# Expert loop of an attention and mixture-of-experts kernel: transposes by a transposing transfer, the row sum by ScalarE

## The chip, the cores and the metric

The kernel runs on one core of a Trainium2 chip. The metric is the device time of one execution in microseconds (us). The engines are TensorE (PE in the profile), VectorE (DVE), ScalarE (ACT), GpSimd (POOL) and SyncE (SP), which here only starts transfers. All run their own instruction streams and meet in semaphores.

## What is computed

Cross attention of 4 x 2048 tokens of 512 features with a short context, a residual, a layer norm, and then one of eight expert matrices for each token, the one with the highest gate score:

```python
x = x + xattn(layernorm(x), ctx_512, ctx_512, Wq, bq, Wk, bk, Wv, bv, Wo, bo)
xn = layernorm(x)
chosen = argmax(xn @ gate_w.T)                    # one of 8 for each token
out = x + xn + xn @ expert_w[chosen].T
```

## The kernel before

A first block prepares weights. A second block takes the tokens in 16 chunks of 512 and does the attention; at its end each token's row is scattered to a DRAM table `rows_by_expert`, sorted by expert, each row with its features, the two factors of its layer norm (`C_RSTD`, `C_NMR`) and its token number (`C_ID`). `row_factors` makes the factors on GpSimd, once a chunk. A third block, from line 1404 on, is the expert loop, which the change rewrites. It runs over 72 tiles (`NTILE`) of 128 rows, each with one expert, unrolled by 8 (`U`, tile t uses slot u = t mod 8). Products keep about fp32 precision by splitting each operand in two fp16 halves, hi and lo, and summing three products (`HL`). For a tile t:

- SyncE (line 1427) waits until the scatter of tile t-8 has landed (`out{u}`), and `load_rows` (lines 736 to 739) reads the tile's first row from the table `tab` in SBUF and starts the load of 128 rows into `row`. The first eight loads are started at the end of the block before.
- VectorE (line 1506) normalises it: `norm` writes `xn2` (printed `xn`) from `row`.
- TensorE (line 1461) transposes the tile in four 128x128 pieces into a PSUM bank (`tbank`, printed `mt`); ScalarE (line 1492) copies that to fp16 as `x2T_hi`; VectorE's `lo` (line 1512) makes `x2T_lo` from the bank less `x2T_hi`.
- TensorE's `mm` multiplies: 4 blocks of the contraction by 3 products, 12 matmuls of 512 columns into `obank2` (printed `mo`).
- GpSimd's `add` (line 1437) makes the row sum row + xn in place.
- VectorE's result (line 1524) is the product times a scale plus that sum, into `res`.
- GpSimd (line 1448) scatters `res` to the output rows by token number.

The order on each engine is that of the code. In its turn for tile t, VectorE does the norm of t+2, the low half of t+1, the result of t; TensorE transposes t+1 and multiplies t; GpSimd sums t+1 and scatters t.

```python
def body(t, k, u):                      # VectorE, before
    if has(t + 2):
        norm(t + 2, k + (u + 2) // U + 1, (u + 2) % U)
    if has(t + 1):
        lo(t + 1, (u + 1) % U)
```

Of the kernel before, what the change touches and what calls it, by code (L numbers as in the profile page):

```python
# [22 lines left out]
ALU = mybir.AluOpType  # L23
# [3 lines left out]
P = 128  # L27
# [6 lines left out]
KT = DM // P  # L34
# [9 lines left out]
VC = DK + 1  # L44
NTOK = B * LQ
REGION = NTOK + P
ROW = DM + 3
C_RSTD, C_NMR, C_ID = DM, DM + 1, DM + 2
NTILE = NTOK // P + E
UNROLL = 8  # L50
SCALE = 1.0 / float(DK) ** 0.5
TOP = 16384.0

# [137 lines left out]
def build(nc, x, ctx, Wq, bq, Wk, bk, Wv, bv, Wo, bo, gate_w, expert_w, out):  # L191
# [89 lines left out]
    slotf = sa("slotf", [P, TPC])  # L281


    low = -(-nc.sbuf_base // 64) * 64
    place = {"q_st": 0, "pp": 32768, "pf": 49152, "cc": 57344, "cT": 65536, "nmT": 73728, "xt3": 75776,
             "experts": 83968, "end": 149504}
    assert low + place["end"] <= nc.sbuf_usable_end
# [2 lines left out]
    def at(name, shape, dt, where, more=0):  # L290
        return nc.alloc_sbuf_tensor_at(name, shape, dt, offset=low + place[where] + more)
# [14 lines left out]
    def row_factors(m, pool, do):  # L306

        par = m.slot % 2
        wait_alone(pool, "ln2_stats", m.n + 1)
        do(nc.gpsimd.tensor_tensor(pay[:, par, :, C_RSTD], ve2[:], pows[:, 0, :], ALU.pow))  # L310
        do(nc.gpsimd.tensor_tensor(mv2[:, :, 1], mv2[:, :, 0], pay[:, par, :, C_RSTD], ALU.mult))
        nc.gpsimd.tensor_scalar(pay[:, par, :, C_NMR], mv2[:, :, 1], -1.0, None, ALU.mult)\
            .then_inc(sem("pay_stats"), 1)
# [1091 lines left out]
    U = UNROLL  # L1405
    with ExitStack() as st:
        xn2 = at("xn2", [P, U, DM], F32, "q_st", 16384)
        x2T = [at(f"x2T_{s}", [P, 2, KT, P], F16, "pf", n * 2048) for n, s in enumerate(("hi", "lo"))]
        res = at("res", [P, U, DM], F32, "pp")
        tbank = [st.enter_context(nc.psum_tensor(f"mt{i}", [P, 512], F32)) for i in range(2)]  # L1410
        obank2 = [st.enter_context(nc.psum_tensor(f"mo{i}", [P, 512], F32)) for i in range(2)]
        blk = st.enter_context(nc.Block())
        assert NTILE % U == 0
# [1 line left out]
        def tiles(eng, body):  # L1415


            with eng.Fori(0, NTILE // U - 1) as k:
                for u in range(U):
                    body(k * U + u, k, u)  # L1420
            for u in range(U):
                body(NTILE - U + u, NTILE // U - 1, u)
# [3 lines left out]

        @blk.sync
        def _(sp):
            with sp.Fori(1, NTILE // U) as k:
                for u in range(U):  # L1430

                    sp.wait_ge(sem(f"out{u}"), 16 * k)
                    load_rows(sp, k * U + u, u)

        @blk.gpsimd
        def _(pool):
            def add(t, u):

                wait_alone(pool, "xn2_ready", t + 1)
                nc.gpsimd.tensor_tensor(row[:, u, 0:DM], row[:, u, 0:DM], xn2[:, u, :], ALU.add)\  # L1440
                    .then_inc(sem("sum_ready"), 1)

            def body(t, k, u):
                if has(t + 1):
                    add(t + 1, (u + 1) % U)

                wait_alone(pool, "res_ready", t + 1 + 2)
                nc.gpsimd.indirect_dma_start(  # L1448
                    out=out_rows, out_offset=bass.IndirectOffsetOnAxis(ap=row[:, u, C_ID:C_ID + 1].bitcast(I32), axis=0),
                    in_=res[:, u, :], in_offset=None, bounds_check=NTOK - 1, oob_is_err=False)\  # L1450
                    .then_inc(sem(f"out{u}"), 16)

            add(0, 0)
            tiles(pool, body)
            for u in range(U):
                wait_alone(pool, f"out{u}", 16 * (NTILE // U))

        @blk.tensor
        def _(pe):
            HL = ((0, 0), (1, 0), (0, 1))  # L1460

            def tr(t, u):
                pe.wait_ge(sem("xn2_ready"), t + 1)
                pe.wait_ge(sem("t_used"), t + 1)
                for k in range(KT):
                    ins = nc.tensor.transpose(tbank[u % 2][:, k * P:(k + 1) * P], xn2[:, u, k * P:(k + 1) * P],  # L1466
                                              ident[:])
                ins.then_inc(sem("t_filled"), 1)

            def mm(t, u):  # L1470
                e = pe.value_load(tab[0:1, 1, bass.ds(t, 1)], min_val=0, max_val=E - 1)
                pe.wait_ge(sem("t_used"), t + 1 + 2)
                pe.wait_ge(sem("res_ready"), t + 1)
                for k in range(KT):
                    for n, (ia, ib) in enumerate(HL):
                        w = e_w[:, bass.ds(e, 1), ib, k, :].rearrange("p a n -> p (a n)")
                        ins = nc.tensor.matmul(obank2[u % 2][:, :], x2T[ia][:, u % 2, k, :], w,  # L1477
                                               start=k == 0 and n == 0, stop=k == KT - 1 and n == 2)
                ins.then_inc(sem("o_filled"), 1)

            def body(t, k, u):
                if has(t + 1):
                    tr(t + 1, (u + 1) % U)
                mm(t, u)

            tr(0, 0)
            tiles(pe, body)

        @blk.scalar
        def _(act):  # L1490
            act.nop().then_inc(sem("o_filled"), 2)

            def body(t, k, u):
                act.wait_ge(sem("t_filled"), t + 1)

                act.wait_ge(sem("o_filled"), t + 1)
                nc.scalar.activation(x2T[0][:, u % 2, :, :], tbank[u % 2][:, :].rearrange("p (k n) -> p k n", k=KT),  # L1497
                                     ACT.Copy).then_inc(sem("t_hi"), 1)

            tiles(act, body)  # L1500

        @blk.vector
        def _(dve):
            dve.nop().then_inc(sem("t_used"), 2)  # L1504
            dve.nop().then_inc(sem("res_ready"), 2)  # L1505

            def norm(t, loads, u):
# [2 lines left out]
                                        row[:, u, C_NMR:C_NMR + 1], ALU.mult, ALU.add).then_inc(sem("xn2_ready"), 1)  # L1510

            def lo(t, u):
                dve.wait_ge(sem("t_hi"), t + 1)
                nc.vector.tensor_tensor(x2T[1][:, u % 2, :, :], tbank[u % 2][:, :].rearrange("p (k n) -> p k n", k=KT),  # L1514
                                        x2T[0][:, u % 2, :, :], ALU.subtract).then_inc(sem("t_used"), 1)

            def body(t, k, u):
                if has(t + 2):
                    norm(t + 2, k + (u + 2) // U + 1, (u + 2) % U)
                if has(t + 1):  # L1520
                    lo(t + 1, (u + 1) % U)
                dve.wait_ge(sem("o_filled"), t + 1 + 2)
                dve.wait_ge(sem("sum_ready"), t + 1)
                nc.vector.scalar_tensor_tensor(out=res[:, u, :], in0=obank2[u % 2][:, :], scalar=inv[:, S_E:S_E + 1],  # L1524
                                               in1=row[:, u, 0:DM], op0=ALU.mult, op1=ALU.add)\
                    .then_inc(sem("res_ready"), 1)

            norm(0, 1, 0)
            norm(1, 1, 1)
            lo(0, 0)  # L1530
            tiles(dve, body)
    attention.close()
    es.close()
# [22 lines left out]
```

## Time and profile before

| | us |
|---|---|
| median of 3 runs | 1072.28 (1070.12 to 1076.3) |
| the profiled execution | 1070.71 |
| its span in the trace | 1068.9 |
| preparation and attention chunks, up to the last block's start | about 827 |
| expert loop, first norm to last result | 836.4 to 1059.7 |

The profile shows busy times by engine, and in forty slices of the span; a trace behind it has each instruction and what it waited for. A matmul's record is longer than the step to the next one, since matmuls overlap; so a tile's cost on TensorE is read from the chain of waits (time from one to the next) and not from the mean of one. "PEclk" is the granted clock of TensorE as a share of its full speed. Instructions of SyncE are listed as SPq, and their time is what the instruction held SyncE, not how long the transfer took; "us to landing" is from the issue to the arrival.

### The profile page before, as it was taken

To read this page: it belongs to the slowest core of one execution; us is meant where nothing else is said; L and a number is where in the kernel's file an instruction comes from. 1 tells how busy PE (TensorE), PEld (TensorE's weight loads), DVE (VectorE), ACT (ScalarE), POOL (GpSimd) and SP (SyncE) were. 2 spreads that over 40 slices of the span, in tenths; PEclk is the share of its full clock that TensorE was granted. 3 is DMA by queue.
4 is the path that set the end of the run, shared out by engine and by line. 5 is a ranking of instruction groups with operands and counts; after the bars stand their busy time and mean duration, and the time that the engine had idled before them with its cause. 6 is when DMAs were issued, how large, how long until landed. Compare 5 with 4: busy or idle time off the path is not lost. (4 is left out here: it accounts for less than half of the span.)

```text
span 1068.9 us, 27389 instructions
## 1 busy us (share of the span) xinstructions
PE 948.5 (89%) x8834; PEld 578.7 (54%) x8835; DVE 817.8 (77%) x1802; ACT 553.4 (52%) x907; POOL 554.1 (52%) x559
## 2 busy tenths in 40 slices
PE   6485799998989999898999999999976699999996
PEld 3342465656656566565665656656564355555553
DVE  7733588899878999897989999888779355566553
ACT  4236775855748567584675855766564121122210
POOL 2412434644555445564455544554555377777774
PEclk9785899999989999998999999999888799999998
DMA  8866626355453544545446255443933456565551
GB/s 240 243 161 174 146 79 157 79 141 120 129 142 91 139 109 125 142 106 142 98 131 166 68 157 119 122 121 82 276 130 120 120 172 169 162 176 170 164 173 35
DMA packets 85687, 149.53 MB, mean 140 GB/s; under 512 B 22849, under 2 KB 24693, under 8 KB 85567
## 3 DMA queue, kind: packets, MB, share of 16 engines
q1 hardware_dynamic: 73359, 111.89, 42.3%
q0 software_dynamic: 11664, 36.05, 8.8%
q8 instruction: 72, 1.18, 0.5%
q14 instruction: 48, 0.39, 0.1%
q10 hardware_dynamic: 544, 0.02, 0.0%
HBM read 58.65 MB, written 40.50 MB: 93 GB/s over the span
## 5 line engine op out<-in xcount | busy, mean ns | idle before, releaser
L827 POOL TENSOR_TENSOR p_lo<-pf,p_hi 77x512 f16<-77x512 f32 x128 | 160.3, 1260 | 194.6 <-ACT p_hi L1171 193.3
L1170 ACT ACTIVATE pf<-scoresT,exp_scale 77x512 f32<-77x512 f32 x256 | 174.9, 683 | 43.9 <-PE scoresT L1005 30.1
L1477 PE MATMUL mo<-e_w,x2T_hi 128*128 x576 | 184.2, 381 | 0.8 <-DVE x2T_lo L1514 0.8
L1171 ACT ACTIVATE p_hi<-scoresT,exp_scale 77x512 f16<-77x512 f32 x256 | 174.8, 683 | 0.0
L1497 ACT ACTIVATE x2T_hi<-mt 128x512 f16<-128x512 f32 x72 | 43.1, 598 | 183.7 <-PE mt L1466 183.7
L827 DVE TENSOR_TENSOR p_lo<-pf,p_hi 77x512 f16<-77x512 f32 x128 | 120.0, 938 | 7.1 <-ACT p_hi L1171 7.1
L1005 PE MATMUL scoresT<-q_st,k_now 97*77 97x512 f32 x256 | 112.4, 472 | 14.5 <-ACT p_hi L1171 11.0
L1524 DVE SCALAR_TENSOR_TENSOR res<-mo,inv,row 128x512 f32<-128x512 f32 x72 | 54.1, 751 | 91.3 <-PE mo L1477 91.3
L1256 DVE TENSOR_REDUCE negmax<-work 128x4 f32<-128x308 f32 x256 | 115.2, 468 | 4.4 <-PE work L1053 2.7
L1151 ACT ACTIVATE xnT_hi<-work 128x512 f16<-128x512 f32 x64 | 37.3, 596 | 146.0 <-PE work L991 145.5
L1477 PE MATMUL mo<-e_w,x2T_lo 128*128 x288 | 109.9, 382 | 0.0
L982 PE MATMUL work<-xnT_hi,wq_hi 128*128 128x512 f16 x256 | 101.3, 396 | 5.5 <-DVE xnT_lo L1234 5.5
L1448 POOL DMA_INDIRECT out<-res,row x72 | 71.5, 994 | 64.9 <-DVE xn L1509 56.7
L1021 PE MATMUL pv<-v_now_hi,p_hi 96*128 96x33 f16 x1024 | 86.7, 179 | 19.4 <-DVE cc L1242 15.9
L982 PE MATMUL work<-wo_hi,cT_hi 128*128 128x512 f16 x256 | 99.0, 387 | 1.9
L982 PE MATMUL work<-xnT_hi,wq_lo 128*128 128x512 f16 x256 | 100.2, 391 | 0.0
L982 PE MATMUL work<-xnT_lo,wq_hi 128*128 128x512 f16 x256 | 99.9, 390 | 0.0
L982 PE MATMUL work<-wo_hi,cT_lo 128*128 128x512 f16 x256 | 97.9, 382 | 0.0
L982 PE MATMUL work<-wo_lo,cT_hi 128*128 128x512 f16 x256 | 97.5, 381 | 0.0
L1021 PEld LDWEIGHTS pv<-v_now_hi,p_hi 96*128 96x128 f16 x1024 | 79.5, 96 | 33.3 <-DVE cc L1242 16.7
L1440 POOL TENSOR_TENSOR row<-row,xn 128x512 f32<-128x512 f32 x72 | 86.3, 1200 | 15.2 <-DVE xn L1509 13.7
L1229 DVE SCALAR_TENSOR_TENSOR q_lo<-work,bq_s,q_hi 128x512 fp32r<-128x512 f32 x64 | 47.9, 749 | 57.8 <-ACT q_hi L1147 57.8
(228 smaller groups left out, 2330.4 us busy)
## 6 DMA issues: line engine op xcount, KB each, us to landing
q_st<-q_hi SPq DMA_DIRECT2D x256, 128.0 KB, 2.4
row<-rows_by_expert SPq DMA_DIRECT2D x72, 257.5 KB, 3.0
xt<-in_x SPq DMA_DIRECT2D x16, 1024.0 KB, 6.3
q_st<-q_lo SPq DMA_DIRECT2D x128, 128.0 KB, 2.5
pay<-in_L_ffn_expert_w SPq DMA_DIRECT2D x8, 1024.0 KB, 7.2
er<-in_L_ffn_expert_w SPq DMA_DIRECT2D x7, 1024.0 KB, 15.4
k_next<-key_stacks SPq DMA_DIRECT2D x5, 462.0 KB, 9.8
key_stacks<-k_nat_hi SPq DMA_DIRECT2D x8, 154.0 KB, 3.3
```

The costliest lines, as they stand in the source:

```text
L827: return tt.tensor_tensor(pp[1][0:LK, g % 2, j, :], pf[:, j, :], pp[0][0:LK, g % 2, j, :], ALU.subtract)
L982: ins = nc.tensor.matmul(dst, a[ia], bm[ib], start=first and n == 0, stop=final and n == 2)
L1005: nc.tensor.matmul(sbank[n % SB][0:LK, :], k_now[0:KR, n, :], q_st[0:KR, n, :], start=True, stop=True)\
L1021: ins = nc.tensor.matmul(obank[h][:, col:col + VC], pp[ip][:, g % 2, j, t * P:(t + 1) * P], v_now[iv][:, g * HG + j, :], start=n == 0, sto ...
L1170: nc.scalar.activation(pf[:, j, :], sbank[n % SB][0:LK, :], ACT.Exp, scale=exp_scale[0:LK, :])
L1171: nc.scalar.activation(pp[0][0:LK, g % 2, j, :], sbank[n % SB][0:LK, :], ACT.Exp, scale=exp_scale[0:LK, :]).then_inc(sem("exp_done"), 1)
L1229: ins = nc.vector.scalar_tensor_tensor(out=q[1][:, at, :], in0=ps[:, :], scalar=bq_s[:, at:at + 1], in1=q[0][:, at, :].bitcast(F32), op0=A ...
L1256: return nc.vector.tensor_reduce(negmax[:, t, g * HG:(g + 1) * HG], ps[:, 0:HG * LK].rearrange("p (j s) -> p j s", j=HG), X, ALU.max, nega ...
L1440: nc.gpsimd.tensor_tensor(row[:, u, 0:DM], row[:, u, 0:DM], xn2[:, u, :], ALU.add)\
L1448: nc.gpsimd.indirect_dma_start(out=out_rows, out_offset=bass.IndirectOffsetOnAxis(ap=row[:, u, C_ID:C_ID + 1].bitcast(I32), axis=0), in_=r ...
L1477: ins = nc.tensor.matmul(obank2[u % 2][:, :], x2T[ia][:, u % 2, k, :], w, start=k == 0 and n == 0, stop=k == KT - 1 and n == 2)
L1524: nc.vector.scalar_tensor_tensor(out=res[:, u, :], in0=obank2[u % 2][:, :], scalar=inv[:, S_E:S_E + 1], in1=row[:, u, 0:DM], op0=ALU.mult, ...
```

## The change

TensorE no longer transposes. ScalarE makes the high half `x2[.., 0, ..]` in fp16 straight from `row` in SBUF (the activation applies the norm's two factors), and the row sum from the same row with the factor rstd + 1, which a fourth extra column (`C_RSTD1`) now carries; it writes the sum to `res`. GpSimd computes that column once a chunk in `row_factors`. VectorE still makes `xn2` and subtracts: the low half `x2[.., 1, ..]`, in SBUF. SyncE then starts one transposing transfer of both halves, 128 partitions x 1024 fp16 (256 KB), from `x2` to `x2T`. Both have four slots (`TB` = 4). In SyncE's turn for tile t stands the transpose of t+3, then the wait for the scatter of t-2 (`LAG` = 2), then the row load of t+6. VectorE's turn is the norm of t+4, the low half of t+3, the result of t, which now adds in place in `res`. ScalarE may write slot t mod 4 once the matmuls of t-4 are done. The rows of the table are 516 instead of 515 numbers long. The first eight tiles are written out ahead of the loop, so that a loop of seven rounds stands between two written-out rounds.

```diff
@@ -44,10 +44,12 @@
-ROW = DM + 3
-C_RSTD, C_NMR, C_ID = DM, DM + 1, DM + 2
+ROW = DM + 4
+C_RSTD, C_NMR, C_ID, C_RSTD1 = DM, DM + 1, DM + 2, DM + 3
...
+TB = 4
+LAG = 2
@@ -281,7 +283,7 @@
-    low = -(-nc.sbuf_base // 64) * 64
+    low = -(-nc.sbuf_base // 32) * 32
@@ -308,6 +310,7 @@
         do(nc.gpsimd.tensor_tensor(pay[:, par, :, C_RSTD], ve2[:], pows[:, 0, :], ALU.pow))
+        nc.gpsimd.tensor_scalar(pay[:, par, :, C_RSTD1], pay[:, par, :, C_RSTD], 1.0, None, ALU.add)
@@ -1405,9 +1408,9 @@
     U = UNROLL
     with ExitStack() as st:
         xn2 = at("xn2", [P, U, DM], F32, "q_st", 16384)
-        x2T = [at(f"x2T_{s}", [P, 2, KT, P], F16, "pf", n * 2048) for n, s in enumerate(("hi", "lo"))]
+        x2 = at("x2", [P, TB, 2, DM], F16, "pf")
+        x2T = at("x2T", [P, TB, 2 * KT, P], F16, "xt3")
         res = at("res", [P, U, DM], F32, "pp")
-        tbank = [st.enter_context(nc.psum_tensor(f"mt{i}", [P, 512], F32)) for i in range(2)]
         obank2 = [st.enter_context(nc.psum_tensor(f"mo{i}", [P, 512], F32)) for i in range(2)]
         blk = st.enter_context(nc.Block())
         assert NTILE % U == 0
@@ -1415,7 +1418,9 @@
         def tiles(eng, body):
 
 
-            with eng.Fori(0, NTILE // U - 1) as k:
+            for u in range(U):
+                body(u, 0, u)
+            with eng.Fori(1, NTILE // U - 1) as k:
                 for u in range(U):
                     body(k * U + u, k, u)
             for u in range(U):
@@ -1426,23 +1431,28 @@
 
         @blk.sync
         def _(sp):
-            with sp.Fori(1, NTILE // U) as k:
-                for u in range(U):
-
-                    sp.wait_ge(sem(f"out{u}"), 16 * k)
-                    load_rows(sp, k * U + u, u)
+            def transpose(t, k, u):
+
+                wait_alone(sp, "x2_lo", t + 1)
+                sp.dma_start(x2T[:, u % TB, :, :], x2[:, u % TB, :, :].rearrange("p h n -> p (h n)"), transpose=True)\
+                    .then_inc(sem(f"x2T_in{u % TB}"), 16)
+
+            def body(t, k, u):
+                if has(t + TB - 1):
+                    transpose(t + TB - 1, k, (u + TB - 1) % U)
+                if isinstance(t, int) and not 0 <= t - LAG < NTILE - U:
+                    return
+                v = (u - LAG) % U
+                wait_alone(sp, f"out{v}", 16 * (k + (u - LAG) // U + 1))
+                load_rows(sp, t - LAG + U, v)
+
+            for t in range(TB - 1):
+                transpose(t, 0, t)
+            tiles(sp, body)
 
         @blk.gpsimd
         def _(pool):
-            def add(t, u):
-
-                wait_alone(pool, "xn2_ready", t + 1)
-                nc.gpsimd.tensor_tensor(row[:, u, 0:DM], row[:, u, 0:DM], xn2[:, u, :], ALU.add)\
-                    .then_inc(sem("sum_ready"), 1)
-
             def body(t, k, u):
-                if has(t + 1):
-                    add(t + 1, (u + 1) % U)
 
                 wait_alone(pool, "res_ready", t + 1 + 2)
                 nc.gpsimd.indirect_dma_start(
@@ -1450,7 +1460,6 @@
                     in_=res[:, u, :], in_offset=None, bounds_check=NTOK - 1, oob_is_err=False)\
                     .then_inc(sem(f"out{u}"), 16)
 
-            add(0, 0)
             tiles(pool, body)
             for u in range(U):
                 wait_alone(pool, f"out{u}", 16 * (NTILE // U))
@@ -1459,49 +1468,38 @@
         def _(pe):
             HL = ((0, 0), (1, 0), (0, 1))
 
-            def tr(t, u):
-                pe.wait_ge(sem("xn2_ready"), t + 1)
-                pe.wait_ge(sem("t_used"), t + 1)
-                for k in range(KT):
-                    ins = nc.tensor.transpose(tbank[u % 2][:, k * P:(k + 1) * P], xn2[:, u, k * P:(k + 1) * P],
-                                              ident[:])
-                ins.then_inc(sem("t_filled"), 1)
-
-            def mm(t, u):
+            def body(t, k8, u):
                 e = pe.value_load(tab[0:1, 1, bass.ds(t, 1)], min_val=0, max_val=E - 1)
-                pe.wait_ge(sem("t_used"), t + 1 + 2)
+                pe.wait_ge(sem(f"x2T_in{u % TB}"), 16 * (k8 * (U // TB) + u // TB + 1))
                 pe.wait_ge(sem("res_ready"), t + 1)
                 for k in range(KT):
                     for n, (ia, ib) in enumerate(HL):
                         w = e_w[:, bass.ds(e, 1), ib, k, :].rearrange("p a n -> p (a n)")
-                        ins = nc.tensor.matmul(obank2[u % 2][:, :], x2T[ia][:, u % 2, k, :], w,
+                        ins = nc.tensor.matmul(obank2[u % 2][:, :], x2T[:, u % TB, ia * KT + k, :], w,
                                                start=k == 0 and n == 0, stop=k == KT - 1 and n == 2)
                 ins.then_inc(sem("o_filled"), 1)
 
-            def body(t, k, u):
-                if has(t + 1):
-                    tr(t + 1, (u + 1) % U)
-                mm(t, u)
-
-            tr(0, 0)
             tiles(pe, body)
 
         @blk.scalar
         def _(act):
-            act.nop().then_inc(sem("o_filled"), 2)
+            act.nop().then_inc(sem("o_filled"), 2 + TB)
 
             def body(t, k, u):
-                act.wait_ge(sem("t_filled"), t + 1)
-
-                act.wait_ge(sem("o_filled"), t + 1)
-                nc.scalar.activation(x2T[0][:, u % 2, :, :], tbank[u % 2][:, :].rearrange("p (k n) -> p k n", k=KT),
-                                     ACT.Copy).then_inc(sem("t_hi"), 1)
+                act.wait_ge(sem(f"row_in{u}"), 16 * (k + 1))
+
+                act.wait_ge(sem("o_filled"), t + 1 + 2)
+                nc.scalar.activation(x2[:, u % TB, 0, :], row[:, u, 0:DM], ACT.Identity,
+                                     scale=row[:, u, C_RSTD:C_RSTD + 1], bias=row[:, u, C_NMR:C_NMR + 1])\
+                    .then_inc(sem("x2_hi"), 1)
+                nc.scalar.activation(res[:, u, :], row[:, u, 0:DM], ACT.Identity,
+                                     scale=row[:, u, C_RSTD1:C_RSTD1 + 1], bias=row[:, u, C_NMR:C_NMR + 1])\
+                    .then_inc(sem("sum_ready"), 1)
 
             tiles(act, body)
 
         @blk.vector
         def _(dve):
-            dve.nop().then_inc(sem("t_used"), 2)
             dve.nop().then_inc(sem("res_ready"), 2)
 
             def norm(t, loads, u):
@@ -1510,24 +1508,26 @@
                                         row[:, u, C_NMR:C_NMR + 1], ALU.mult, ALU.add).then_inc(sem("xn2_ready"), 1)
 
             def lo(t, u):
-                dve.wait_ge(sem("t_hi"), t + 1)
-                nc.vector.tensor_tensor(x2T[1][:, u % 2, :, :], tbank[u % 2][:, :].rearrange("p (k n) -> p k n", k=KT),
-                                        x2T[0][:, u % 2, :, :], ALU.subtract).then_inc(sem("t_used"), 1)
+                dve.wait_ge(sem("x2_hi"), t + 1)
+                dve.wait_ge(sem("xn2_ready"), t + 1)
+                nc.vector.tensor_tensor(x2[:, u % TB, 1, :], xn2[:, u, :], x2[:, u % TB, 0, :], ALU.subtract)\
+                    .then_inc(sem("x2_lo"), 1)
 
             def body(t, k, u):
-                if has(t + 2):
-                    norm(t + 2, k + (u + 2) // U + 1, (u + 2) % U)
-                if has(t + 1):
-                    lo(t + 1, (u + 1) % U)
-                dve.wait_ge(sem("o_filled"), t + 1 + 2)
+                if has(t + TB):
+                    norm(t + TB, k + (u + TB) // U + 1, (u + TB) % U)
+                if has(t + TB - 1):
+                    lo(t + TB - 1, (u + TB - 1) % U)
+                dve.wait_ge(sem("o_filled"), t + 1 + 2 + TB)
                 dve.wait_ge(sem("sum_ready"), t + 1)
                 nc.vector.scalar_tensor_tensor(out=res[:, u, :], in0=obank2[u % 2][:, :], scalar=inv[:, S_E:S_E + 1],
-                                               in1=row[:, u, 0:DM], op0=ALU.mult, op1=ALU.add)\
+                                               in1=res[:, u, :], op0=ALU.mult, op1=ALU.add)\
                     .then_inc(sem("res_ready"), 1)
 
-            norm(0, 1, 0)
-            norm(1, 1, 1)
-            lo(0, 0)
+            for t in range(TB):
+                norm(t, 1, t)
+            for t in range(TB - 1):
+                lo(t, t)
             tiles(dve, body)
     attention.close()
     es.close()
```

On SyncE, in the loop: before, one tile's turn is

```order
L738 ISA [waits out3]
L738 TENSOR_LOAD tab
L738 ISA x2
L739 ISA
L739 DMA row<-rows_by_expert 128x515
```

and now, with `x_10803` the tile `x2`,

```order
L1437 DMA_TRANSPOSE x2T<-x_10803 128x8x128 [waits x2_lo]
L741 ISA [waits out3]
L741 TENSOR_LOAD tab
L741 ISA x2
L742 ISA
L742 DMA row<-rows_by_expert 128x516
```

The transpose, with its wait for VectorE's low half, stands ahead of the wait for the scatter and ahead of the row load.

On VectorE, in the loop: before, one turn is

```order
L1509 TENSOR_SCALAR xn_10794<-row 128x512 [waits row_in4]
L1514 TENSOR_TENSOR x2T_lo<-mt,x2T_hi 128x512 [waits t_hi]
...
L1524 SCALAR_TENSOR_TENSOR res<-mo,inv,row 128x512 [waits sum_ready,o_filled]
```

and now two turns are

```order
L1507 TENSOR_SCALAR xn_10802<-row 128x512 [waits row_in1]
L1513 TENSOR_TENSOR x_10803<-xn_10802,x_10803 128x512 [waits xn2_ready,x2_hi]
L1521 REGISTER_ALU
L1523 SCALAR_TENSOR_TENSOR res<-mo,inv,res 128x512 [waits sum_ready,o_filled]
L1507 TENSOR_SCALAR xn_10802<-row 128x512 [waits row_in2]
L1513 TENSOR_TENSOR x_10803<-xn_10802,x_10803 128x512 [waits xn2_ready,x2_hi]
L1521 REGISTER_ALU
L1523 SCALAR_TENSOR_TENSOR res<-mo,inv,res 128x512 [waits sum_ready,o_filled]
```

The order of the three kinds is the same. What they wait for differs, and the norm is now four tiles ahead of the result of its turn instead of two, the low half three instead of one.

## Rows read from the trace of the kernel before

**Rows 1.** Busy time of each engine by window; the windows of the expert loop and around.

```profile
core 0: us, PE busy (x) PEld busy (x) DVE busy (x) ACT busy (x) POOL busy (x), PEclk, DMA share, GB/s
760.00:800.00 40.00, 33.12 (x428) 25.37 (x427) 30.93 (x68) 27.23 (x47) 21.39 (x25) 0.83 0.63 226
800.00:815.00 15.00, 12.56 (x82) 7.12 (x81) 13.04 (x46) 5.33 (x8) 7.17 (x8) 1.00 0.29 109
...
840.00:845.00 5.00, 5.00 (x18) 2.18 (x17) 1.02 (x2) 0.12 (x1) 0.00 (x0) 0.65 0.00 0
...
850.00:1050.00 200.00, 200.00 (x1059) 108.56 (x1057) 119.16 (x198) 39.48 (x66) 145.09 (x134) 1.00 0.56 167
```

**Rows 2.** Chain of waits, 740 to 900 and 1050 to 1069: start, us, what.

```profile
836.34 0.09 issue
836.43 0.56 DVE xn L1509
836.98 0.04 issue
837.03 1.13 PE mt L1466 x4
838.16 0.02 issue
838.18 0.61 ACT x2T_hi L1497
838.78 0.02 issue
838.81 0.70 DVE x2T_lo L1514
839.51 0.32 issue
839.83 4.57 PE mo L1477 x12
844.41 0.44 PE mt L1466 x4
844.84 2.59 PE mo L1477 x12
847.43 0.44 PE mt L1466 x4
...
1053.68 5.19 PE mo L1477 x24
```

**Rows 3.** Groups of instructions by line, 850 to 1050: busy us, mean ns, idle before.

```profile
L1440 POOL TENSOR_TENSOR row<-row,xn 128x512 f32<-128x512 f32 x67 | 80.4, 1200 | 1.5
L1448 POOL DMA_INDIRECT out<-res,row x67 | 66.6, 994 | 54.2 <-DVE xn L1509 49.1 <-issue 5.0
...
L1524 DVE SCALAR_TENSOR_TENSOR res<-mo,inv,row 128x512 f32<-128x512 f32 x66 | 49.6, 751 | 80.6 <-PE mo L1477 80.6
L1514 DVE TENSOR_TENSOR x2T_lo<-mt,x2T_hi 128x512 f16<-128x512 f32 x66 | 45.1, 683 | 0.0
```

**Rows 4.** SyncE: line 739 and its landings, the first eight loads, scatter waits and landings.

```profile
L739 SPq DMA_DIRECT2D row<-rows_by_expert x72: 337/338/368, 827.4 to 1040.5; - x72
DMA to landing us min/median/max: 2.5/3.0/4.1
827.35 8.12 SPq L739 DMA_DIRECT2D row<-rows_by_expert  x8
SPq L738 <- DMA out<-res,row: 111.2, 48, 3.7
out<-res,row POOLq DMA_INDIRECT x67, 2.9
```

**Rows 5.** Other transfers that SyncE starts: ns min/median/max, their landings (us).

```profile
L401 SPq DMA_DIRECT2D bvec<-in_L_xattn_bv x1: 1135/1135/1135, 2.8 to 2.8; - x1
L401 SPq DMA_DIRECT2D bvec<-in_L_xattn_bo x1: 819/819/819, 4.0 to 4.0; - x1
L401 SPq DMA_DIRECT2D bvec<-in_L_xattn_bq x1: 2747/2747/2747, 4.8 to 4.8; - x1
DMA to landing us min/median/max: 5.5/7.4/8.7
L868 SPq DMA_DIRECT2D q_st<-q_hi x256: 585/597/1938, 64.3 to 752.0; - x128
q_st<-q_hi SPq DMA_DIRECT2D x256, 128.0 KB, 2.4
```

**Rows 6.** DMA queues, 850 to 1050: packets, MB, share of sixteen engines.

```profile
q1 hardware_dynamic: 9216, 16.88, 35.2%
q0 software_dynamic: 5280, 16.46, 21.2%
issues: line engine op xcount, KB each, median us to landing
row<-rows_by_expert SPq DMA_DIRECT2D x64, 257.5 KB, 2.9
```

**Rows 7.** Single lines (ns min/median/max) and one wait, whole span.

```profile
L1509 DVE TENSOR_SCALAR xn<-row x72: 536/539/566, 836.4 to 1050.9; 128x512 f32<-128x512 f32 x72
L1120 ACT ACTIVATE xn<-xt,nmr,rstd x60: 797/809/817, 70.3 to 703.3; 128x512 f32<-128x512 f32 x60
L827 DVE TENSOR_TENSOR p_lo<-pf,p_hi x128: 669/678/2653, 90.0 to 783.8; 77x512 f16<-77x512 f32 x128
L312 POOL TENSOR_SCALAR pay<-mv x16: 231/232/245, 181.2 to 817.5; 128x4 f32<-128x4 f32 x16
POOL pay L310 <- DVE ve L1362: 92.8, 14, 7.7
```

**Rows 8.** Timeline of TensorE at the loop's start: start, us, line, operation.

```profile
840.23 0.63 PE L1477 MATMUL mo<-e_w,x2T_lo 128*128 x1
840.66 1.06 PE L1477 MATMUL mo<-e_w,x2T_hi 128*128 x2
841.51 0.63 PE L1477 MATMUL mo<-e_w,x2T_lo 128*128 x1
```

## The prediction

> **What bounds the kernel now.** First the windows [rows 1]. From 850 to 1050 us, TensorE is busy 200.00 of 200 us at a granted clock of 1.00 (2.4 GHz), and VectorE 119, ScalarE 39, GpSimd 145 us: the expert loop is TensorE's alone. Then the chain of waits [rows 2]. It goes back through the loop without one gap: 4 transposes (0.44 us), 12 matmuls (2.59 us), and again, 3.03 us a tile. Where no transpose is left, two tiles take 5.19 us, 2.59 each. So the change takes off 0.44 us of TensorE a tile, at most 71 x 0.44 = 31 us, if nothing else becomes the bound. Then what runs beside it: the groups by line [rows 3] and SyncE [rows 4]. SyncE waits 111 us in 48 waits for scatters to land, so it has room, and a row tile is asked for as soon as its slot is free. A slot is freed some 4.6 us after its tile's last matmul (result, GpSimd's turn, landing), so the row for eight tiles on is asked for some four tiles before VectorE reads it, and a landing of about 3 us costs nothing. This last point is what the change alters.
>
> **TensorE's part.** 288 transposes go, with the ScalarE copy and the VectorE subtraction that read them from PSUM. The 12 matmuls stay. Floor: 2.59 us a tile, 10 of 72 tiles surely near it (the first eight have their rows already; the last have none to wait for): 10 x -0.44 = -4.4 us.
>
> **ScalarE, VectorE, GpSimd.** ScalarE makes two tiles from the row, each at most 0.81 us (the activation with scale and bias columns from SBUF [rows 7]): 1.6 us a tile, under any period below. VectorE keeps three instructions, 0.54 + 0.68 + 0.75 = 1.97 us [rows 3, 7]. The subtraction now reads SBUF; the same form with an SBUF source took 0.68 [rows 7], so I keep it. GpSimd loses 1.20 us a tile and only scatters, 0.99. None of them becomes the bound. The sum `row + xn` as one activation costs nothing that anything waits for: it is ready two to three tiles before the result needs it. GpSimd's extra small instruction in the chunks (0.23 us each, 16 times, by its twin [rows 7]) hides in GpSimd's 93 us of waiting for VectorE's statistics [rows 7]; only the last one delays the last scatter and the first row load: +0.2 us.
>
> **SyncE's part, where the forecast is decided.** Each tile SyncE now starts a transpose, then waits for a scatter, reads a table entry, and starts a row load, in that order. Two things follow.
>
> (1) *A ring.* The transpose of tile t+3 waits for VectorE's low half of t+3. Behind it on SyncE stands the row load of t+6. VectorE reads that row (norm of t+6) two turns later and, in its own order, just ahead of the low half of t+5, and the transpose of t+5 waits for that. So two tiles cannot take less than: SyncE's time in the transpose instruction (call it h) + the way to the row load's issue + its landing + norm + low half + hand-overs. The way to the issue is 0.76: eight row loads span 8.12 us from the first issue to the last's end, (8.12 - 0.34) / 7 = 1.11 each, less the issue's 0.34 [rows 4]. Landing is 3.0 in the median, 2.5 to 4.1 [rows 4]. Norm 0.54, low half 0.68 [rows 7, 3]. Three hand-overs at about 0.05, as between the chain's first links [rows 2]: 0.15. Without h that is 5.13 us. The ring equals today's 3.03 us a tile at h = 6.06 - 5.13 = 0.93 us. The wait for the scatter of t-2 doesn't add: its result follows the low half of t+1 on VectorE, two turns (6.1 us and more) ahead of the transpose of t+3, and needs 0.75 and a landing of 2.9 [rows 3, 4], so it has landed over 2 us before SyncE asks.
>
> (2) *h itself.* No row shows a transposing transfer. Bounds: below, the plain row load of the same 256 KB, 0.34 us. Above, a transfer cut into many small pieces. The transpose must address 128 x 8 pieces of 256 bytes; the nearest rows by number of pieces are the three bias vectors, 512 pieces each, which held SyncE 0.82, 1.14 and 2.75 us [rows 5]. A copy between SBUF places of 64 pieces (32 partitions, two each) held it 0.60 [rows 5]. I take the mean of the three, 1.57, since the count of pieces and not the bytes sets these rows apart (0.34 for 257.5 KB, 1.14 for 2 KB). Then the ring is (1.57 + 5.13) / 2 = **3.35 us a tile**. SyncE's own load is 1.57 + 1.11 = 2.68, less than that.
>
> On the price of such a transfer the Trainium skill speaks twice. Its page "Advanced Engine Details and Errata", X-Bar Transpose (TRN2), has transposing transfers as fast as regular ones; by that h would be 0.34 and the fast rival below would hold. The same page of the Trainium skill, DMA Advanced Topics, calls the hardware queue's transpose efficiency "Worse"; that speaks for the forecast. No row here tells them apart.
>
> **Start and end.** Today the first matmul stands 3.40 us after the first norm (836.43 to 839.83) [rows 2]. After: four norms 2.16, one low half 0.68, then the first landing. An SBUF-to-SBUF copy lands in 2.4 with h = 0.60 [rows 5], so 3.4 with h = 1.57: 6.3 us, +2.9. Both begin at TensorE's low clock (0.65 in the mean of 840 to 845 [rows 1]; the first tile takes 4.57 us either way). The end is as before: last result, scatter, landing.
>
> **Sum**, against the profiled execution's own 1070.71 us (span 1068.9): 62 tiles x (3.35 - 3.03) = +19.8; ten tiles -4.4; start +2.9; GpSimd +0.2; together +18.5, 1089.2. That execution stood 1.6 under the median of the runs, so **1091 us**.
>
> **Rivals.**
> *Fast: the transpose is issued like a copy* (faster than before). It decides from h below 0.93. At h = 0.60 the ring is 5.73 / 2 = 2.86: 62 x -0.17 = -10.5, -4.4, start +1.9, +0.2: -12.8, 1060 on the median. At 0.34 with a landing of 2.9 it is 2.69: -21.1 - 4.4 + 2.1 = -23.4, 1049. Below that the DMA engines hold: per tile the row loads take 35.2% of 200 us over 64 = 1.10 us of all sixteen, the scatters 21.2% over 67 = 0.63 [rows 6], a transpose of as many bytes about 1.10 if it costs as a load does, together 2.83. For it: SyncE's waits show that a plain issue leaves room. Against it: the three bias rows. Chance 0.18.
> *Slow: h at the upper row.* At 2.75 the ring is 3.94 and SyncE alone 3.86, so both agree: 62 x 0.91 = +56.4, -4.4, start +4.0, +0.2: 1128. With the landing at its longest, 4.1, since three streams now share the engines, 4.49: 1162. For it: sixteen engines at 2.83 of 3.35 us are 84% used against 56% now [rows 1], so landings get longer, not shorter. Chance 0.20.
> *Clock.* TensorE now stands 0.76 of 3.35 us. If the granted clock falls for stretches, a tile takes up to 5.1 (twelve at 0.43, the step between matmuls at 1.2 GHz [rows 8]) and is the bound itself. One tile in eight so: 9 x 1.75 = +16, 1107. Rows speak both ways: at 84% busy the clock stayed 1.00 (800 to 815), at 83% it was 0.83 (760 to 800) [rows 1]. Chance 0.08.
> *One transpose at a time.* If a transpose were worked off block by block and the next waited for it, the landing is the period. The many-piece rows landed in 7.4 us in the median [rows 5]: 72 x 4.4 = +315, 1387. The Trainium skill, "VectorE: DVE Perf Modes", The three transpose paths, gives 1309 ns for one 128x128 block; eight would be 10.5 us, and by that the time would be some 1610. Nothing in this trace bears it out. Chance 0.04.
>
> **How the numbers follow.** Forecast 0.50 (h 0.9 to 2.2, 1072 to 1110), fast 0.18, slow 0.20, clock 0.08, one at a time 0.04. Over or under 0.5% (5.4 us) is about what a measurement of this kernel can tell from no change. Of the forecast's half, 0.05 lie within that and 0.02 below it, so faster 0.20, same 0.05, slower 0.75. The range leaves out the lower third of the fast case and the upper half of the slow one with the last: 1052 to 1150.
>
> **What the changed kernel's profile would show.** Right: the TensorE groups show the matmuls alone, 72 x 12, with idle time in front of them put down to the transposing transfer; SyncE's time in the transpose near 1.6 us; the row load issued within 1 us of the transpose's end; VectorE idle ahead of the norm, waiting for the row load, and no longer ahead of the result; the same pattern each two tiles, 6.7 us apart. Wrong: TensorE unbroken at 2.59 a tile (h small, or rows that come earlier than I count); or SyncE never waiting, so that its own instructions are the bound (h above 2.8); or the granted clock below 1.00 in the loop; or gaps in the attention chunks, where I count nothing. What would make the forecast wrong above all is h, which I have from transfers of another kind.

## The result and the profile after

The changed kernel takes 1104.89 us (median of 4 runs, 1097.27 to 1107.31) against 1071.20 beside it: 1.030 times the time of before, 95% interval 1.023 to 1.037. It is slower by 34 us; the forecast was 1091, 19 us slower, with a range of 1052 to 1150. Ratios leave out disturbed executions, which concerns one run in this document (the 1075.77 us among the eight of the version with every second tile).

The windows of the changed kernel (us; busy time and count of each engine, granted clock, DMA share, GB/s), to be held against [rows 1]:

```profile
core 0: us, PE busy (x) PEld busy (x) DVE busy (x) ACT busy (x) POOL busy (x), PEclk, DMA share, GB/s
...
860.00:1060.00 200.00, 160.93 (x702) 64.44 (x700) 103.40 (x172) 87.36 (x116) 58.09 (x58) 0.99 0.90 223
```

TensorE is busy 161 of 200 us instead of all 200, with its clock at 0.99 (its upper level, 2.4 GHz), and the DMA engines are busy 0.90 of the time instead of 0.56. 58 scatters in 200 us make 3.45 us a tile, where the kernel before needs 3.03. The DMA engines' share times this pace, 0.90 x 3.45 = 3.10 us, is what they spend on a tile; that product is used again below.

Its chain of waits in the middle of the loop (start, us, what), to be held against the unbroken PE rows of [rows 2]:

```profile
949.52 1.27 SPq L1437
950.78 0.05 issue
...
950.89 0.06 SPq L741
950.99 0.60 SPq L741
951.62 0.15 SPq L741
...
952.04 3.03 DMA row<-rows_by_expert
955.12 0.07 issue
955.23 0.05 issue
955.30 0.25 issue
955.55 0.70 DVE x L1513
956.28 0.05 issue
956.33 1.26 SPq L1437
```

This is the ring, link by link: SyncE starts a transpose (line 1437, 1.27 us); reads the table (line 741); starts the row load, which lands 3.03 us later; VectorE makes the norm (its record runs from 955.09 to 955.64; in the chain the short pieces and the 0.25 stand for it) and the low half; and SyncE starts the transpose two tiles on. From 949.52 to 956.33 are 6.81 us for two tiles. TensorE doesn't occur in these links. In the chain of the whole loop its matmuls make up 7%, at the start, at the end and once near 964.

Who waits for whom, same stretch (us in total, times, longest):

```profile
POOL out L1458 <- DVE res L1523: 142.4, 58, 3.7
ACT x L1492 <- DMA row<-rows_by_expert: 110.0, 56, 3.1
DVE xn L1507 <- DMA row<-rows_by_expert: 95.8, 57, 2.8
...
PE mo L1478 <- DVE res L1523: 36.0, 34, 1.8
PE mo L1478 <- DMA x2T<-x: 2.7, 2, 2.2
```

VectorE now waits 95.8 us for row loads, which cost it nothing in the loop before, and no longer for TensorE (80.6 us in [rows 3]). TensorE waits for VectorE's results, since these stand behind the norms in VectorE's order; the transposed tiles themselves are there in time (2.7 us).

SyncE waits for little, and only for VectorE's low half:

```profile
SPq L208 <- DVE x L1513: 19.4, 30, 1.2
```

So SyncE's own turn takes (200 - 19.4) / 58 = 3.11 us. The ring, at 3.45, is the bound, but SyncE and the DMA engines (3.10) stand close below it, and both above the 3.03 of the kernel before.

The added instructions (ns min/median/max), SyncE's and ScalarE's:

```profile
L1437 SPq DMA_TRANSPOSE x2T<-x x72: 1232/1268/1476, 845.0 to 1086.4; - x72
DMA to landing us min/median/max: 3.1/3.5/5.4
...
L741 SPq TENSOR_LOAD <-tab x72: 264/615/962, 832.4 to 1078.5; - x72
...
L1492 ACT ACTIVATE x<-row x72: 797/813/817, 842.4 to 1083.8; 128x512 f16<-128x512 f32 x72
```

### The profile page after: what moved, and what is told of

Its sections match the earlier page's. It is cut to its first block and busy times, and to the rows that moved or that the text cites. A ratio compares the mean times of both kernels' runs of the same rounds, so it can differ in the third digit from the quotient of the medians.

```text
span 1103.8 us, 26830 instructions
## 1 busy us (share of the span) xinstructions
PE 925.5 (84%) x8546; PEld 533.6 (48%) x8547; DVE 818.7 (74%) x1802; ACT 619.4 (56%) x979; POOL 472.5 (43%) x503
## 5 line engine op out<-in xcount | busy, mean ns | idle before, releaser
L1478 PE MATMUL mo<-e_w,x2T 128*128 x864 | 200.0, 385 | 61.1 <-DVE res L1523 40.2
L1478 PEld LDWEIGHTS mo<-e_w,x2T 128*128 128x128 f16 x864 | 80.4, 99 | 180.6 <-issue 95.8
L1492 ACT ACTIVATE x<-row 128x512 f16<-128x512 f32 x72 | 58.5, 813 | 142.9 <-DMA row<-rows_by_expert 123.6
L1507 DVE TENSOR_SCALAR xn<-row 128x512 f32<-128x512 f32 x72 | 39.4, 551 | 115.4 <-DMA row<-rows_by_expert 107.5
L1024 PE MATMUL pv<-v_now_lo,p_hi 96*128 96x33 f16 x1024 | 85.8, 178 | 0.0
```

Source lines behind the costliest of these rows:

```text
L1024: ins = nc.tensor.matmul(obank[h][:, col:col + VC], pp[ip][:, g % 2, j, t * P:(t + 1) * P], v_now[iv][:, g * HG + j, :], start=n == 0, sto ...
L1478: ins = nc.tensor.matmul(obank2[u % 2][:, :], x2T[:, u % TB, ia * KT + k, :], w, start=k == 0 and n == 0, stop=k == KT - 1 and n == 2)
L1492: nc.scalar.activation(x2[:, u % TB, 0, :], row[:, u, 0:DM], ACT.Identity, scale=row[:, u, C_RSTD:C_RSTD + 1], bias=row[:, u, C_NMR:C_NMR ...
```

## Experiments

### The row load one tile less ahead

```diff
-LAG = 2
+LAG = 3
```

> The same number the other way: the row load in SyncE's turn for t is that of t+5. Ring theory: the ring spans one tile, 6.8 us a tile instead of 3.4, 64 x 3.4 = +218, about 1320 us, the DMA engines half idle. Rival, the DMA engines or SyncE are the bound: the same transfers and instructions, about 1105 to 1120.

It took 1301.81 us in its one run, where the ring theory had about 1320 and the rival 1105 to 1120. Its chain:

```profile
942.87 1.27 SPq L1437
...
944.44 0.61 SPq L741
...
945.52 2.65 DMA row<-rows_by_expert
...
948.65 0.70 DVE x L1513
949.38 0.05 issue
949.43 1.27 SPq L1437
```

The same links, 6.56 us, now for one tile instead of two. The rival is out: the instructions and transfers are the same, the DMA engines are busy 0.47 of the time, and the time is 197 us more. Only where the row load stands in SyncE's order has changed. TensorE's granted clock is 0.76 in the mean there (860 to 1060 us), but TensorE isn't the bound: it stands waiting for VectorE's results for 73.6 of 200 us. The DMA engines' time a tile is unchanged, 0.47 x 6.67 = 3.13 us.

### The low half ahead of the norm on VectorE

```diff
             def body(t, k, u):
-                if has(t + TB):
-                    norm(t + TB, k + (u + TB) // U + 1, (u + TB) % U)
                 if has(t + TB - 1):
                     lo(t + TB - 1, (u + TB - 1) % U)
+                if has(t + TB):
+                    norm(t + TB, k + (u + TB) // U + 1, (u + TB) % U)
```

> In VectorE's turn the low half of t+3 stands ahead of the norm of t+4, nothing else is changed. Ring theory: the transpose of t+5 then no longer stands behind the norm that waits for the row of t+6; the ring runs over the low half of t+6 and spans three tiles, and the time falls as with the load one tile farther ahead, to some 3.1 us a tile and 1083 us. Rival, DMA engines or SyncE the bound: about 1105. If VectorE's order did not matter, 1105 too.

1089.00 us (1085.3 to 1092.4), 1.017 of before (1.014 to 1.020), 16 us under the changed kernel, where the theory had 1083 and the rivals 1105. Two exchanged instructions take back half of the loss, so the order on VectorE was part of the cause. What is left is another bound; its chain is SyncE's alone:

```profile
949.56 1.25 SPq L1437
950.92 0.06 SPq L741
951.02 0.61 SPq L741
951.66 0.15 SPq L741
951.81 0.05 issue
951.88 0.05 issue
952.02 0.44 SPq L742
952.61 0.24 issue
952.84 0.06 SPq L1423
953.02 1.27 SPq L1437
```

SyncE waits 1.9 us in 200 us, and one of its turns takes 3.17 us in the mean (200 us for 63 row loads; the turn shown is a long one): 1.27 for the transpose, 0.35 for the row load, the rest the table's reading and what lies between. That alone is more than TensorE's 3.03 of before. The DMA engines are at 0.98 there, 3.11 us a tile:

```profile
860.00:1060.00 200.00, 174.01 (x762) 69.66 (x761) 112.86 (x189) 95.32 (x127) 62.00 (x63) 1.00 0.98 244
```

### The row load one tile farther ahead

```diff
-LAG = 2
+LAG = 1
```

> One number is changed: in SyncE's turn for tile t stands the load of the row for t+7 instead of t+6. Ring theory: the ring of transpose, row load, landing, norm, low half and transpose (6.8 us in the changed kernel's chain) then spans three tiles instead of two, 2.3 us a tile, and no longer binds. The next bound is the DMA engines, busy 0.90 of 200 us for 58 tiles, 3.1 us a tile, or SyncE's own 1.27 + 1.25 + 0.35 = 2.9: from 3.45 to about 3.1 a tile, 64 x -0.35 = -22, some 1083 us, VectorE no longer idle for the row load. Rival, the DMA engines are the bound already at 0.90 busy: no change, about 1105.

1101.08 us (1098.4 to 1104.0), 1.027 of before (1.024 to 1.030): 4 us less where 22 were expected, and no gain clear of noise, since the changed kernel's interval is 1.023 to 1.037. By the time alone this is the rival's case (no change, about 1105); the chain tells them apart. The ring is gone from its chain, which is SyncE's own as above (SyncE waits 1.0 us in all), but a turn of SyncE takes 3.39 us:

```profile
944.44 1.37 SPq L1437
945.87 0.05 issue
945.92 0.06 SPq L741
946.01 0.89 SPq L741
946.94 0.15 SPq L741
...
947.35 0.46 SPq L742
947.83 1.25 SPq L1437
```

The transposes hold SyncE 1.39 us in the median (2.13 at most) and the table reads 0.70. So the expectation was right that the ring would open, and wrong that the next bound lay at 3.1. Why the same instructions take SyncE 3.39 us here and 3.17 with VectorE's order changed isn't settled: the DMA engines are nearly full in both (0.93 and 0.98), at the same price a tile (3.15 and 3.11 us), and which of the two holds the other these runs don't tell. That the ring was what held the changed kernel rests on the two experiments above, and not on this one.

### Row loads by GpSimd

The low half first, and in the loop `load_rows` is called by GpSimd behind its scatter, so that SyncE only starts transposes. The row load is also one tile farther ahead.

```diff
-LAG = 2
+LAG = 1
...
                 nc.gpsimd.indirect_dma_start(
...
                     .then_inc(sem(f"out{u}"), 16)
+                v = (u - LAG) % U
+                wait_alone(pool, f"out{v}", 16 * (k + (u - LAG) // U + 1))
+                load_rows(pool, t - LAG + U, v, "late_row_in")
```

> Low half ahead of the norm, and the row loads of the loop are started by GpSimd behind its scatter (tile t+7 in the turn of t) instead of by SyncE, which only starts transposes, 1.3 us a tile. Theory A, SyncE's instructions are the bound of the version with the low half first: the time falls from 1089 toward TensorE's 2.6 to 2.9 us a tile, 1050 to 1070. Theory B, the sixteen DMA engines are (0.98 busy at 3.17 us a tile): it stays at 3.1 us a tile, 1085 to 1095.

1117.00 us (1107.8 to 1119.1), 1.040 of before (1.035 to 1.045): neither theory's time. SyncE now waits 106.8 of 180 us for VectorE, so it isn't the bound, and the tile takes 3.75 us:

```profile
860.00:1040.00 180.00, 138.96 (x585) 56.48 (x583) 86.61 (x144) 72.43 (x97) 78.65 (x97) 0.95 1.00 207
...
q0 software_dynamic: 7683, 24.50, 50.8%
...
row<-rows_by_expert POOLq DMA_DIRECT2D x48, 258.0 KB, 5.1
```

The row loads land in 5.1 us instead of 3.0, the DMA engines show a share of 1.00 at 207 GB/s, less than the 244 above, and VectorE waits 93 of 180 us for the rows (87 of 200 with the low half first alone). A share of 1.00 at 3.75 us is more than the 3.11 above for the same bytes, so the price a tile depends on who starts the transfers. With all of SyncE's starts as they were it didn't move: 3.10, 3.13, 3.11 and 3.15 us a tile in the changed kernel and the three experiments above, at shares from 0.47 to 0.98. This run therefore doesn't decide between the theories. Which resource binds the version with the low half first stays open between SyncE (its turn, without its waits, 3.14 us) and the DMA engines (3.11); its 3.17 lie close to both.

### Half a transpose

The low half isn't transposed, and the product that needs it takes the high half instead, so this part of the computation is left out.

```diff
-                sp.dma_start(x2T[:, u % TB, :, :], x2[:, u % TB, :, :].rearrange("p h n -> p (h n)"), transpose=True)\
+                sp.dma_start(x2T[:, u % TB, 0:KT, :], x2[:, u % TB, 0, :], transpose=True)\
...
-            HL = ((0, 0), (1, 0), (0, 1))
+            HL = ((0, 0), (0, 0), (0, 1))
```

> The changed kernel with only the high half transposed, 512 fp16 a partition instead of 1024; the low half is made but not used, its product is done with the high half instead (that part of the computation is left out). If SyncE's time in the transposing transfer goes by its pieces it is about 0.65 us and the ring (6.8 - 0.6 - some 0.4 of landing) / 2 = 2.9 to 3.1 us a tile, about 1075; if it is a fixed price it stays at 1.27 and the ring at 3.3 to 3.4, about 1100. The DMA engines' share falls from 0.90 to 0.6 or 0.7 either way.

1091.07 us in one run, between the two cases (1075 and 1100). Half the pieces hold SyncE 1.22 us instead of 1.27:

```profile
L1437 SPq DMA_TRANSPOSE x2T<-x x72: 977/1222/1327, 841.3 to 1071.8; - x72
```

So in the median it is nearly a fixed price between these two sizes and doesn't go by pieces. The ring went from 6.8 to 6.2 us for two tiles (transposes at 940.82 and 947.03 in its chain) by its other links: the table read is 0.33 us in the median and a landing near there 2.7. Over 200 us the pace is 3.33 us a tile (60 scatters), as the fixed price had it. The DMA engines fell to 0.71, 2.37 us a tile.

### ScalarE's sum alone

The kernel before, with ScalarE's sum and the fourth extra column; TensorE transposes.

```diff
+                act.wait_ge(sem(f"row_in{u}"), 16 * (k + 1))
+                nc.scalar.activation(res[:, u, :], row[:, u, 0:DM], ACT.Identity,
+                                     scale=row[:, u, C_RSTD1:C_RSTD1 + 1], bias=row[:, u, C_NMR:C_NMR + 1])\
+                    .then_inc(sem("sum_ready"), 1)
```

> The kernel before with one part of the change alone: ScalarE makes the row sum from the row with the factor rstd + 1, rows of 516 numbers, GpSimd only scatters; TensorE still transposes. Theory: TensorE stays the bound at 3.03 us a tile, within 2 us of before, 1069 to 1073. Rival: longer rows, the extra GpSimd instruction in the chunks or the ScalarE sum cost something (the last block began 6 us later in the profile of the changed kernel than in that of before): 1077 or more, the first row load near 833 instead of 827.

1075.35 us over 10 runs, 1.0027 of before (1.0005 to 1.0050), 3.4 us by the medians: more than the 2 us that were allowed for, less than the rival's 1077. The loop is what it was: from the first norm (843.75) to the last result's end (1066.59) 222.8 us, before 223.2. TensorE is busy 200.00 of 200 us. What is lost in the profiled execution lies ahead of the loop.

### Longer rows alone

```diff
-ROW = DM + 3
+ROW = DM + 4
```

> The kernel before with rows of 516 numbers instead of 515 (the last one zero) and tiles placed at multiples of 32 instead of 64 bytes, nothing else. ScalarE's sum alone stood 0.3% over before. If the longer rows or the placing cost that, this stands 3 us over before too; if the extra GpSimd instruction in each chunk does, it is the same as before within 1 us.

1.0001 of before (0.9976 to 1.0026). The longer rows cost nothing that could be measured, and neither does the placing at multiples of 32 bytes, which this run has too. That leaves the GpSimd instruction in `row_factors` for the 3 us, or chance; the last experiment looks at it once more.

### Every second tile by the transposing transfer

Even tiles as in the change, odd ones over TensorE's transposes and the PSUM bank as before, the low half ahead of the norm, ScalarE's sum for all.

```diff
             def body(t, k, u):
-                if has(t + TB - 1):
-                    transpose(t + TB - 1, k, (u + TB - 1) % U)
+                if u % 2 and has(t + TB - 1):
+                    transpose(k * (U // 2) + (u + TB - 1) // 2, (u + TB - 1) % U)
...
             def body(t, k8, u):
+                if u % 2 == 0:
+                    tr(t + 1, k8 * (U // 2) + u // 2, u + 1)
                 e = pe.value_load(tab[0:1, 1, bass.ds(t, 1)], min_val=0, max_val=E - 1)
```

> Even tiles go by the transposing transfer, odd ones by TensorE's transposes and the PSUM bank as before; SyncE's turn is that of the changed kernel, VectorE's has the low half ahead of the norm. Theory (with the transfer on each tile SyncE's own instructions and the DMA engines are full at 3.17 us a tile once the ring is opened, each with the transfer's 1.3 us in it): half the transfers leaves SyncE at 2.5 and the DMA engines at 2.5 us a tile, TensorE at 2.59 + 0.22 = 2.81 is the bound: 72 x -0.22 = -16, start +2, rows and the extra GpSimd instruction +3: about 1061 us, TensorE without a gap. Rival (SyncE's reads and the landings grow beside any transposing transfer, whoever else transposes): TensorE waits, 3.0 us a tile or more, 1072 or more.

1067.19 us over 8 runs, 0.993 of before (0.990 to 0.996), and in its second series of 12 runs, beside the next version, 1067.58:

> The version with every second tile transposed by TensorE, unchanged, again beside the one without the column: 1067 us, 0.993 of before, on another chip or at another time.

0.9947 there (0.9921 to 0.9974). So it is faster than both kernels, by half a per cent against the one before; 1061 had been expected. TensorE is the bound again, 178 of 180 us, at 2.86 us a tile (63 in 180 us) where 2.81 were worked out:

```profile
860.00:1040.00 180.00, 178.02 (x886) 88.46 (x884) 116.93 (x188) 88.78 (x127) 62.61 (x63) 1.00 0.92 224
```

SyncE's own turn is at the 2.5 us expected (it waits 22.5 of 180 us). The DMA engines stand at 0.92, 2.63 us a tile where 2.5 were worked out. The loop is 9.1 us shorter than before (842.61 to 1056.67, 214.1 us); the start and the gaps take the rest of the 16.

### The same without the extra column

```diff
-        nc.gpsimd.tensor_scalar(pay[:, par, :, C_RSTD1], pay[:, par, :, C_RSTD], 1.0, None, ALU.add)
...
+                nc.scalar.activation(rstd1[:, u:u + 1], row[:, u, C_RSTD:C_RSTD + 1], ACT.Copy, bias=1.0)\
+                    .then_inc(sem("rstd1"), 1)
```

> The version with every second tile transposed by TensorE, but without the extra column: rows are 515 numbers again, GpSimd's extra instruction in the chunks is gone, and ScalarE adds 1 to rstd in the loop (a small activation of about 0.2 us and a wait a tile, ScalarE is half idle there). Theory (the GpSimd instruction, 16 x 0.23 us at the chunk boundaries where the next chunk's work on GpSimd stands behind it, is what sets the kernel with ScalarE's sum alone 0.3% over before, since longer rows alone cost nothing): 3 us less than the run beside it, about 1064 us, 0.990 of before. Rival: the 0.3% were chance or the loop's own: the same as the run beside it.

1064.30 us over 6 runs, 0.9921 of before (0.9890 to 0.9952), the lowest median here. It is 3.3 us under the one beside it by the medians, as expected, but the intervals of the two overlap. Three comparisons of times point the same way (this one, ScalarE's sum alone, the longer rows alone); none of them is beyond doubt by itself. The traces don't settle it: the profiled first norm stands at 836.43, 838.63 and 838.99 us in the three kernels without the column's instruction, and anywhere from 838.58 to 843.75 in the nine with it. That the GpSimd instruction costs 3 us is likely and not shown.

## Why the prediction was right, and where it was off

**The ring was right.** The prediction said which engines' orders close it and that it spans two tiles. The chain bears this out, and so do two experiments that move it: one tile less ahead makes it span one tile, and the time a tile nearly doubles; VectorE's exchanged order opens it, and half of the loss is gone.

**Its terms, two tiles.** The transpose's hold on SyncE was put at 1.57 us and is 1.27. The way from its end to the row load's issue was put at 0.76 and is 1.26 (950.78 to 952.04). The landing was put at 3.0 and is 3.0. Norm, low half and hand-overs were put at 1.37; from the landing (955.07) to the next transpose (956.33) are 1.26. The sum was 6.70 and is 6.81. Two errors nearly cancelled, and that is luck: with the transpose as measured and all else as forecast, the ring would be (1.27 + 5.13) / 2 = 3.20 us a tile and the time some 9 us over before instead of 19. The way's term came from [rows 4], eight plain loads one behind the other; behind a transposing transfer the table read alone takes 0.62 us where it took 0.27. Mostly for this reason SyncE's own turn, put at 2.68, is 3.11. The DMA engines' time a tile, put at 2.83 with a transpose priced like a load, is 3.10. Both lie above the 3.03 of before, so opening the ring alone was not enough to gain.

**How h, SyncE's time in the transpose, was found was wrong, though its range held it.** "Since the count of pieces and not the bytes sets these rows apart" doesn't hold for this transfer: half the pieces cost 1.22 us, all of them 1.27. The bias rows, of another kind and started beside a dozen others, were a bound and not a measure. That transposing transfers are as fast as regular ones (the Trainium skill, "Advanced Engine Details and Errata", X-Bar Transpose (TRN2)) doesn't hold here for the issue, 1.27 against 0.34 us for as many bytes, and for the landing only nearly, 3.5 against 3.0.

**The size, 34 us instead of 19.** The loop, first norm to last result, grew from 223.2 to 252.1 us: +28.9 where the sum had +18.3. These rows of VectorE's timeline give the pace (the results of the fourth, the sixty-seventh and the last tile):

```profile
861.21 0.75 DVE L1523 SCALAR_TENSOR_TENSOR res<-mo,inv,res 128x512 f32<-128x512 f32 x1 [0.78 <-PE mo L1478]
...
1076.84 0.74 DVE L1523 SCALAR_TENSOR_TENSOR res<-mo,inv,res 128x512 f32<-128x512 f32 x1
...
1093.80 0.75 DVE L1523 SCALAR_TENSOR_TENSOR res<-mo,inv,res 128x512 f32<-128x512 f32 x1 [1.84 <-PE mo L1478]
```

63 tiles in 215.6 us are 3.42 each, +0.39 x 63 = +25, where the step "62 tiles x (3.35 - 3.03)" had +19.8; the mis-sized term is the ring, by 0.07 a tile. In the two tiles shown the way to the issue is +0.50, the transpose -0.30, norm and what follows -0.11. The step "ten tiles surely near the floor" was too kind: the first three steps are at 2.59, but the last five tiles take 17.0 us, 3.4 each, where six or seven more had been put at the floor: the last rows come through the ring too. Together these eight are +0.5 in place of most of the -4.4. The start was right: TensorE's first matmul stands 6.1 us after the first norm (848.48, 842.41), 6.3 forecast. The rest lies ahead of the loop: the first norm stands 6.0 us later in the profiled execution (842.41, 836.43), where the forecast had 0.2 for GpSimd's extra instruction, hidden in its 93 us of waiting. ScalarE's sum alone stood 3.4 us over before, so some 3 us of this may be that instruction; what delays the loop's start isn't shown, and starts differ by 5 us among kernels with the same attention chunks.

**The engines.** ScalarE's two activations take 0.81 and 0.80 us, as bounded; VectorE and GpSimd are no bound, as forecast. The low half from SBUF takes 0.685 us. The clock rival fell out in the changed kernel: the granted clock was 0.99 with TensorE busy 161 of 200 us.

**The signs.** SyncE's time in the transpose (1.27 us), VectorE idle ahead of the norm and not ahead of the result, and the pattern each two tiles (6.8 us) came much as forecast. Two signs did not: the row load is issued 1.26 us behind the transpose's end and not within 1, and TensorE's waits are put to VectorE's results (36.0 us) and hardly to the transposing transfer (2.7).

**The rivals.** Fast needed h below 0.93; h is 1.27. Slow needed h near 2.75 or row landings of 4.1; neither came (3.2 at most). One at a time is refuted at the loop's start, where nothing holds the transposes back. The first two and the next two:

```profile
L1437 SPq DMA_TRANSPOSE x2T<-x x2: 1272/1320/1369, 845.0 to 846.5; - x2
DMA to landing us min/median/max: 3.3/3.3/3.4
...
L1437 SPq DMA_TRANSPOSE x2T<-x x2: 1281/1284/1287, 847.9 to 849.3; - x2
DMA to landing us min/median/max: 3.2/3.2/3.3
```

They are issued 1.4 us apart and each lands 3.2 to 3.4 us later, so none waits for the one before it to land. The Trainium skill, "VectorE: DVE Perf Modes", The three transpose paths, gives 1309 ns for one block. That can't be a price per block here, as eight blocks land in 3.5 us all told.

## What to carry to other kernels

When work is moved from the bounding engine to a queue, write down in what order that queue and the engines around it take their turns, and follow one item until it meets itself again: the sum of that ring, divided by the tiles it spans, is a floor that no share of busy time shows. The cheapest remedy was an order (low half before norm), worth 16 us; the second was to give the new path only a part of the tiles, every second one, which beat both kernels. Before opening a ring, work out the floors right behind it: here SyncE's own turn and the DMA engines' time a tile, both 3.1 us, were already above the 3.03 of the kernel before.

## What the runs showed of the hardware that was not expected

- A transposing transfer, SBUF to SBUF, holds SyncE 1.27 us for 256 KB and 1.22 us for 128 KB, and lands in 3.5 us; a plain load of as many bytes holds it 0.34 to 0.35.
- SyncE's read of one table entry takes 0.27 us in a row of plain loads, 0.62 with transposing transfers between them, 0.33 with transfers half as large.
- The DMA engines' share times the pace is a steady price for the same transfers from the same engines: 3.10, 3.15, 3.13 and 3.11 us a tile at paces of 3.45, 3.39, 6.67 and 3.17. It is 2.37 with half a transpose, 2.63 with every second tile transposed so, about 1.7 in the kernel before, and 3.75 for the same bytes with the row loads started by GpSimd.
- Transposing transfers overlap: four issued 1.4 us apart land 3.2 to 3.4 us after their issues.
- A row load started by GpSimd beside scatters and transposes lands in 5.1 us, by SyncE in 3.0.
